# The second half's attention products in four column tiles of 32, with four key tiles added up on GpSimd

## What is computed

```
x = x + attention(layernorm(x))      # rotary Q, K; causal softmax(Q K^T / sqrt(32)) V; output projection Wo, bo
x = x + ffn(layernorm(x))            # silu(x Wg^T * gs) * (x Wu^T * us), then Wd^T * ds; inner size 1408
```

## Time and profile before

| | us |
|---|---|
| median of 3 runs (757.69, 758.27, 768.73) | 758.27 |
| profiled execution, its own time | 768.15 |
| its span | 766.4 |
| TensorE busy in it | 743.2 (97%) |
| VectorE / ScalarE / GpSimd busy | 438.5 / 307.4 / 247.0 |
| line 1240 (P with v), TensorE busy | 141.6 |

### The profile page before, as it was taken

The page is one execution under the profiler, slowest core; times in us unless marked ns, Lnnn a source line. Parts: engine busy times, 40 slices in busy tenths (PEclk is TensorE's granted clock), DMA queues, the critical chain, the costliest instruction groups (busy, mean ns, idle before and its releaser), DMA issues.

```text
span 766.4 us, 10665 instructions
## 1 busy us (share of the span) xinstructions
PE 743.2 (97%) x3563; PEld 539.6 (70%) x3563; DVE 438.5 (57%) x1103; ACT 307.4 (40%) x641; POOL 247.0 (32%) x224
## 2 busy tenths in 40 slices
PE   7999999989999999999999999999999999999996
PEld 7888888755555556566546547787788888888884
DVE  7978765895775767677767726773324114214112
ACT  3323132265664656566646564222332222223221
POOL 0815153311113141414231426932223223224223
PEclk9999999989999999999999999999999999999998
DMA  8677468643665666667656556670001001001001
GB/s 279 228 268 261 172 259 269 248 140 101 170 170 144 166 163 169 171 166 183 170 143 166 139 161 159 231 321 1 0 1 56 0 1 55 0 0 56 0 1 57
DMA packets 54318, 104.39 MB, mean 136 GB/s; under 512 B 14820, under 2 KB 18404, under 8 KB 53748
## 3 DMA queue, kind: packets, MB, share of 16 engines
q1 hardware_dynamic: 54264, 103.72, 44.3%
HBM read 69.62 MB, written 38.21 MB: 141 GB/s over the span
## 4 chain that ended last, share of the span: by engine, by line
PE 84%; DMA 4%; issue 4%; DVE 2%; POOL 2%; ACT 2%; SPq 1%; DVEq 0%; POOLq 0%; ACTq 0%
PE ps L1101 37%; PE ps L1240 17%; PE ps L1126 9%; PE ps L1316 9%; PE ps L1219 9%; DMA q_st<-neg_max_T 3%; PE ps L1093 2%; POOL hid_lo L592 1%; PE ps L1160 1%; ACT o_raw L687 1%; ACT p L680 1%; DMA l_cols<-o_raw 1%; SPq L421 0%; PE ps L1137 0%; DMA rec_l<-rec_rows 0%
## 5 line engine op out<-in xcount | busy, mean ns | idle before, releaser
L680 ACT ACTIVATE p<-ps 128x384 f32<-128x384 f32 (+3 forms) x384 | 160.7, 487 | 74.8 <-PE ps L1219 74.2
L841 DVE CUSTOM_DVE_ANT_0 masked<-ps,mask_qk 128x512 bf16<-128x512 f32 (+1 forms) x240 | 114.4, 503 | 80.3 <-PE ps L1126 79.0
L1219 PE MATMUL ps<-q_st,k_st 99*128 99x384 f32 (+2 forms) x384 | 136.4, 373 | 6.0 <-DMA q_st<-neg_max_T 4.9
L1240 PE MATMUL ps<-p,v_slot 128*64 128x512 f32 (+3 forms) x768 | 141.6, 506 | 0.2 <-ACT o_raw L687 0.2
L1126 PE MATMUL ps<-k_st,q_st 96*128 96x512 f32 (+2 forms) x384 | 132.3, 366 | 2.0 <-DVE row_max L841 1.7
L1052 DVE SCALAR_TENSOR_TENSOR hid<-ps,us_sb,silu 128x512 f32<-128x512 f32 x44 | 33.0, 751 | 165.3 <-PE ps L1101 159.6
L592 POOL TENSOR_TENSOR hid_lo<-hid,hid_hi 128x512 fp32r<-128x512 f32 x44 | 56.7, 1289 | 172.4 <-ACT hid_hi L756 172.4
L561 POOL TENSOR_SCALAR_AFFINE_SELECT p<-p 128x512 f32<-128x512 f32 x64 | 40.8, 642 | 215.4 <-ACT p L680 215.4
L1240 PEld LDWEIGHTS ps<-p,v_slot 128*64 128x64 f32 x768 | 51.3, 140 | 78.0 <-issue 65.4
L1126 PEld LDWEIGHTS ps<-k_st,q_st 96*128 96x128 f32 x384 | 72.7, 190 | 32.4 <-issue 21.8
L1219 PEld LDWEIGHTS ps<-q_st,k_st 99*128 99x128 f32 x384 | 72.9, 191 | 25.3 <-ACT p L680 8.9
(11 more groups left out here) (119 smaller groups left out, 1074.2 us busy)
## 6 DMA issues: line engine op xcount, KB each, us to landing
qk_scratch<-st_hi SPq DMA_DIRECT2D x32, 512.0 KB, 3.8
q_st<-qk_scratch SPq DMA_DIRECT2D x32, 384.0 KB, 4.4
k_st<-qk_scratch SPq DMA_DIRECT2D x32, 384.0 KB, 5.1
flag_st<-in_ffn SPq DMA_DIRECT2D x32, 264.0 KB, 2.8
ffn_copy<-in_ffn SPq DMA_DIRECT2D x32, 264.0 KB, 3.4
qk_scratch<-st_lo SPq DMA_DIRECT2D x16, 512.0 KB, 3.9
o_T<-o_raw SPq DMA_DIRECT2D x32, 128.0 KB, 4.8
rec_l<-rec_rows SPq DMA_DIRECT2D x32, 128.0 KB, 3.3
```

The costliest lines, as they stand in the source:

```text
L680: act.activation(p32[:, at:at + q0 + w - keep], ps[:, ST_BANK + i % ST_RING, keep - q0:w], ACT.Exp, scale=SCALE).then_inc(exp_done, 1)
L841: ins = dve.tensor_tensor_reduce((masked_a if u < 2 else masked)[:, s_before(i) % 2, col:col + kept], scores, mask_qk[:, 512 - kept:512], ...
L1219: pe.matmul(ps[:, ST_BANK + i % ST_RING, 0:w], k_st[0:K_ALL, slot, kt * P:(kt + 1) * P], q_st[0:K_ALL, slot, q0:q0 + w], start=True, stop= ...
L1240: ins = pe.matmul(ps[VW * a:VW * (a + 1), o_bank(u, half), q0 - 512 * half:512], v_slot[:, slot, kt, :], p32[:, at:at + n], start=(kt == 0 ...
```

## The change

What is computed stays the same. Group 0 is untouched. The second half of the queries is cut into quarters of 256 (part 1: 512..767, part 2: 768..1023) and every product there uses 32 stationary columns, so that both heads take four column tiles: for head a of the pair, one tile for v (rows 64a to 64a+31) and one for ones (rows 64a+32 to 64a+63).

- In the tile of ones, the key tiles 0..3 are no longer multiplied one by one: GpSimd adds them up for queries 512..1023 (`sum_p`, three additions of 128x512 for each head, into p_sum, three slots) and one product with ones takes the sum.
- The tile of ones has then room: v of key tiles 4, 5 (part 1) and 6, 7 (part 2) is multiplied there, into the columns 256..511 of the bank ("w"). ACT copies it out with the rest, two more DMAs for each pair (o_w) bring it to the partitions of o_T, and `scale_group` adds it before it multiplies.
- Columns of moving data for each column tile: group 0 1280 (as before), group 1 1024 (part 1; before 1024), group 2 768, group 3 768 (part 2; before 1152 each).
- A pair is evacuated in three parts (entry 3 and entry 9 of the even step, entry 9 of the odd one). Group 1 waits for `p_summed` and `p_high_masked`.
- rec_l is gone: the reciprocals of groups 0..6 are loaded into o_T's last group (7), so `move_pair(14)` waits for `o_scaled` 7.
- wo is loaded behind step 30's other DMAs instead of in stage A.

```diff
+PV_GROUPS = [
+    (0, [[("vl", 0)], [("vl", 1)], [("vl", 2)], [("vl", 3)]]),
+    (1, [[("v", 0), ("w", 4)], [("v", 1), ("l", None)], [("v", 2), ("l", 4)], [("v", 3), ("l", 5)], [("w", 5)]]),
+    (2, [[("v", 0), ("w", 6)], [("v", 1), ("l", None)], [("v", 2), ("l", 4)]]),
+    (2, [[("v", 3), ("l", 5)], [("v", 4), ("l", 6)], [("v", 5), ("l", 7)], [("w", 7)]]),
+]
...
+            def output_product(u, a, part, kind, kt):
...
+                row = VW * a
+                if kind == "vl":
+                    rows, weights, col = slice(row, row + VW), v_slot[:, slot, kt, :], q0 - q_low
+                elif kind == "v":
+                    rows, weights, col = slice(row, row + D), v_slot[:, slot, kt, 0:D], q0 - q_low
+                elif kind == "l":
+                    rows, weights, col = slice(row + D, row + VW), v_slot[:, slot, 0, D:VW], q0 - q_low
+                else:
+                    rows, weights, col = slice(row + D, row + VW), v_slot[:, slot, kt, 0:D], QW + q0 - q_low
+                ins = pe.matmul(ps[rows, bank, col:col + q_end - q0], weights, probs, ...
...
+                for products in rounds:
                     for a in range(2):
-                        slot = (2 * u + a) % SLOTS
...
+                        for kind, kt in products:
+                            output_product(u, a, part, kind, kt)
...
             for t in range(HEADS):
                 copy_v(t)
                 if t % 4 == 0 and t >= 8:
                     scale_group((t - 8) // 4)
-                mask_p(t)
+                mask_low(t)
+                sum_p(t)
+                mask_high(t)
...
+            def sum_p(t):
...
+                pool.tensor_tensor(total, second_half(0), second_half(1), ALU.add).then_inc(p_sum_step, 1)
+                pool.wait_ge(p_sum_step, 2 * t + 1)
+                pool.tensor_tensor(total, total, second_half(2), ALU.add).then_inc(p_sum_step, 1)
+                pool.wait_ge(p_sum_step, 2 * t + 2)
+                pool.tensor_tensor(total, total, second_half(3), ALU.add).then_inc(p_summed, 1)
...
             def scale_group(g):
                 pool.wait_ge(rec_in, 64 * (g + 1))
-                pool.tensor_tensor(o_T[:, g, :], o_T[:, g, :], rec_l[:, :], ALU.mult).then_inc(o_scaled, 1)
+                pool.tensor_tensor(o_T[:, g, S // 2:S], o_T[:, g, S // 2:S], o_w[g % 2][:, :], ALU.add).then_inc(o_joined, 1)
+                pool.wait_ge(o_joined, g + 1)
+                pool.tensor_tensor(o_T[:, g, :], o_T[:, g, :], rec_of(g), ALU.mult).then_inc(o_scaled, 1)
...
             def move_pair(u):
-                sp.wait_ge(o_evac, 2 * u + 2)
+                sp.wait_ge(o_evac, PARTS * (u + 1))
...
+                if u == PAIRS - 2:
+                    sp.wait_ge(o_scaled, GROUPS - 1)
                 for a in range(2):
...
+                    sp.dma_start(o_w[t // 4 % 2][rows, :], o_raw[l_rows, u % 2, S:S + 2 * QW]).then_inc(o_moved[u % 2], 16)
...
+                if t == HEADS - 2:
+                    sp.wait_ge(st_ps, NPC * t)
+                    sp.dma_start(wo_st[:, :, :], wo).then_inc(wo_in, 16)
```

More of the change, by code:

```diff
@@ L96 @@
 TEST_AFTER = (3, 3)
[L97 to L101 removed]
+PV_GROUPS = [
[4 rows of a table added]
+]
+assert len(PV_GROUPS) == len(PV_AFTER[0]) + len(PV_AFTER[1])
+PV_FIRST = {("vl", 0, 0), ("v", 1, 0), ("w", 1, 4), ("v", 2, 0), ("w", 2, 6)}
+PV_LAST = {("vl", 0, 3), ("v", 1, 3), ("l", 1, 5), ("w", 1, 5), ("v", 2, 5), ("l", 2, 7), ("w", 2, 7)}
+PARTS = 3
+PART_DONE = (2, 4, 4)
+QW = 256
+SUM_KT = KT // 2
+SUM_SLOTS = 3
 FFN_COLS = KC * INTER
@@ L159, in transformer_block @@
             xst_c = sb("xst_c", [P, TJ, H], F32, after_wo)
-        wo_st = sb("wo_st", [P, KC, H], F32)
+        p_sum = sb("p_sum", [P, SUM_SLOTS, S // 2], F32)
+        o_w = [sb(f"o_w{k}", [P, S // 2], F32) for k in range(2)]
         with ExitStack() as after_v:
@@ L273, in transformer_block @@
         p_high_masked = sem("p_high_masked")
-        pv_half = [sem(f"pv_half{k}") for k in range(2)]
+        p_sum_step = sem("p_sum_step")
+        p_summed = sem("p_summed")
+        p_sum_read = sem("p_sum_read")
+        pv_part = [sem(f"pv_part{k}") for k in range(PARTS)]
         o_evac = sem("o_evac")
@@ L279, in transformer_block @@
         rec_in = sem("rec_in")
+        o_joined = sem("o_joined")
         o_scaled = sem("o_scaled")
@@ L338, in t_bank, with o_bank, rec_of @@
             return MM_BANK + j if n == N_CH else T_BANK + (j + 2) % TJ
-        def o_bank(u, half):
-            return ST_BANK if (u, half) == (PAIRS - 1, 1) else O_BANK
+        def o_bank(u, part):
+            return (O_BANK, ST_BANK + 2, ST_BANK)[part] if u == PAIRS - 1 else O_BANK
+        def rec_of(g):
+            return o_T[:, GROUPS - 1, :] if g < GROUPS - 1 else rec_last[:, :]
         def next_tiles(c, j):
```

111 lines of the change are left out of this document (67 added, 44 removed).

## The result

| | before | changed |
|---|---|---|
| median of four runs each | 758.15 | 779.85 |
| profiled execution, its span | 766.4 | 772.9 |
| TensorE / VectorE / GpSimd busy in it | 743.2 / 438.5 / 247.0 | 732.5 / 469.4 / 381.8 |

The ratio of the runs (of their means; one run of the kernel before is at 768.73) is 1.0248, with a 95% interval of 1.0199 to 1.0296: slower by 2.0 to 3.0%, where 749 us were forecast (1.2% faster) and the range ended at 769. TensorE has 10.7 us less to do, as the first part of the page says, and the kernel is slower all the same.

The account below looks back on a forecast made before the run. TensorE, busy 743.2 of 766.4 us, was taken as the bound, with the chain at stage B's end tied to it. -18.5 + 0.5 + 3 + 5.6 = -9.4 from 758.27 gave 749 us; range 738 to 769.

Parts of the forecast that it names:

- Part 1: Stage B's products on TensorE: four column tiles side by side shorten 14 odd steps, -18.5 us; added matmul starts +0.5.
- Part 2: GpSimd's three additions a head in stage B: 4.05 us a head, hidden with 3.9 us to spare, costed at nothing.
- rival 2: Stage B: four wide, but late DMAs, clock dips and GpSimd's additions holding up VectorE add 8 to 20 us; chance 0.17.
- Part 3: SP and DMAs in stage B's six scaling steps: two more issues a pair delay the row maxima, +3 us, bounds 0 to 12.
- Part 4: Tail after step 31: pair 14's move waits for group 6's scaling, chunk 2 starts later, +5.6 us, bounds +2 and +8.
- the difference of 9.9: Whole kernel: the runs' median lies 9.9 us below the profiled 768.15, so the sum was added to 758.27.
- Rival 1: Stage B's products: only two streams run at a time, four tiles share their rate, about 807 us; chance 0.2.

Follow-up runs that it names:

- the version with o_w later and pieces: Changed kernel, group 6's reciprocals in own memory, everything at old addresses, o_w's moves issued behind row maxima, GpSimd's two-input operations in 256-column pieces: 754.03 us beside 760.97.
- the pieces: Changed kernel with only GpSimd's two-input operations cut into pieces of 256 columns: 772.29 us beside 761.13.
- the two later versions: Same 256-column pieces in two reworked kernels: o_w moved behind row maxima (754.03 us); additionally reciprocals' loads split and join a step before multiplication (752.68 us).
- the two repeated profiles: Kernel before and changed kernel, both unedited, profiled once more: 759.94 us and 779.42 us, with profiled spans 759.2 and 780.9.
- o_w's moves: Changed kernel without the two o_w moves of 64 KB for each pair from pair 4 on: 771.85 us beside 760.84.
- the halves: Kernel with o_w's moves behind the row maxima, its four reciprocals' loads split two and two over successive steps, scaling one step later: 762.39 us beside 761.25.
- the version with the join first and without the sums: Kernel with reciprocals' loads split, join one step ahead of multiplication, and GpSimd's sums left out from head 3 on: 761.04 us beside 761.40.
- the version with group 6 apart: Changed kernel with group 6's reciprocals in the dead half of v_sb, so move_pair(14) waits only for group 5's scaling: 774.12 us beside 760.23.

## Why the prediction was wrong

- **Part 1, the products (-18.5 + 0.5): right, four tiles run side by side.** Group 1 1.87 us forecast, 1.86 measured; groups 2 and 3 1.43, 1.44; plain odd steps 7.96, 8.05 to 8.08, so 14 x 1.21 = 16.9 of 18.5. In the version with o_w later and pieces, stage B is 278.8 us against 295.2: the gain is there. One argument for it goes further than its rows: the kernel writes one product for each head, and in which order the compiled program holds the two passes of a product no record shows. The times exclude that the tiles wait for each other, not that the passes start in program order.
- **Part 2, GpSimd's additions "hidden": this step failed.** Their time was right (4.0 us a head for 4.05) and so was the room; what was costed at nothing is what they do to VectorE. I had the mechanism in rival 2, but looked for it in VectorE's share of busy time (6.9 of 9.28), where it doesn't show: a 0.17 us operation becomes 0.4 to 1.25, on the way to the row maxima. By the pieces it is some 7 of the 21.7 us in the changed kernel, and 7.7 and 11.4 in the two later versions, where the intervals leave no doubt.
- **Part 3, the scaling steps (+3, bounds 0 to 12): mis-sized.** The even ones rose by 8.0 us (3.7 to 11.7) between the two repeated profiles, 3.8 (6.4 to 10.2) between the first ones. SP's two issues are in it as forecast: 0.6 us a step, 3.5 in six, and they go with o_w's moves. The rest is the landing, which went from 3.5 to 4.5 us in the repeated profiles and from 4.1 to 4.3 in the first ones; it differs that much between executions of one kernel, so how much of it the change added is open. That the landing hangs on the bytes queued ahead is shown by the halves (3.1 us). What was priced wrongly is the spare time: a plain step has 1.4 us between the landing and the next product, and with a landing of 4 us nothing of it is left, so each delay counts in full. The odd steps behind them, +12.0 (+4.4 in the first profiles), stood in no term: a wait there comes from VectorE, goes with the pieces, and the clock falls behind both.
- **Part 4, the tail (+5.6): mechanism right, size off.** +7.7 in the first profiles, +8.2 in the others: issues and landings fit, but group 1's wait is 3.4 for 1.2, joining and multiplying 4.5 for 3.7, by GpSimd's operations beside VectorE's. The 6 us of idle time ahead of chunk 2 are not there as forecast: they are spread over group 1, chunk 1 and chunk 2.
- **The place in SBUF: no term at all.** The diff showed the pad and the new tensors, and nothing in the profile of before can price it: +5 to 6 us. Nor was there a term for stage A's other 3 us, which come with a half-speed stretch at 9.4 to 9.8 us (last section).
- **The sum against the profile of before: the difference of 9.9 was carried over, and hid something.** The first execution had 13.7 us at half clock, the repeated one 3.4; (13.7 - 3.4) / 2 = 5 us, an estimate, of the 7.2 between their spans. So the median to which the sum was added has few waits in it, while the five waits that part 3 scaled up from are those of the longer execution (4.9 us in all; two waits, 2.4 us, in the repeated one).
- **Rival 1** is refuted by the rows above. **Rival 2** was the case, and its upper end of 769 was too low: it had nothing for the place, for stage A and for the odd steps, and priced one dip of 1.7 us a scaling step, where the repeated profile has eight stretches, three of them 6.8 us long.

## What to carry to other kernels

Where GpSimd gets two-input work, ask not whether VectorE has time but which of VectorE's short SBUF operations stand on a critical chain, and keep GpSimd's instructions short. Price a wait on TensorE with the half-speed stretch that may follow it, and take the level to add to from several executions. Keep tensors that the change doesn't touch at their addresses. For a small DMA on a critical chain add up both, its issue and its landing behind what is queued ahead of it: once the spare time is used up, each of them counts in full.

## What the runs showed of the hardware

- The address of the operands sets the pace of full matmuls: 0.2267 us from start to start, 0.2333 when all behind xT stands 1856 bytes higher; 389, 394 and 397 ns a record at three places. Products with xU, which moved along with the weights, stayed at 389 to 391. Which distances are bad is open.
- Five 128x8 operations of VectorE took 2.26 to 2.27 us beside a GpSimd multiplication with 2.23 to 2.24 us to go, in the version with the join first and without the sums; alone they take 0.17.
- One broadcast DMA with an outermost dimension of 4 landed its 512 KB some 11 us after its issue; four DMAs of 128 KB had all landed 5.2 to 6.0 us after the first was issued.
- The row maxima's DMAs of 4 KB land 1.75 us after their issue in a plain step and 2.2 to 5.9 us after it in the scaling steps of the two repeated profiles, behind the reciprocals' 512 KB and the pair's moves.
- In the profiles of the changed kernel, of its repetition and of the version with group 6 apart a half-speed stretch starts at 9.4 to 9.8 us, in none of the first three of the kernel before; in later runs of both sides it came and went (with the stretch stage A ends at 158 to 160, without it at 155 to 157). What decides it is open. It costs more than itself: in both profiles of the changed kernel one of VectorE's splits of the weights then falls beside GpSimd's two-input work and takes 3.44 instead of 1.19 us.
